# Stages 6 and 7 in one block: one pass for two norms, projections issued ahead of the last group's norm, and output and final norm per batch in rows of tokens

## The reference

```python
x = _layernorm(x + _L3_attn_ref(x, ...))     # stage 6
x = _layernorm(x + _L3_ffn_ref(x, ...))      # stage 7

# stage 6, _L3_attn_ref: 6 layers
for i in range(6):
    xn = ln(x, ln1_w[i], ln1_b[i])
    x = linear_attn(xn @ wq[i], xn @ wk[i], xn @ wv[i]) @ wo[i] + bo[i] + x
    xn = ln(x, ln2_w[i], ln2_b[i])
    x = leaky_relu(xn @ w1[i]) @ w2[i] + x

# stage 7, _L3_ffn_ref: q, k, v from the norm of x; tokens in quarters of 64 per batch,
# quarter e uses the first 128 / 2**e channels of its input
xn = ln(xe, norm_w, norm_b)                   # a norm of a value that was normed just before
q, k, v = (xn[..., :m] @ w[:, :m].T + b for w, b in ...)
attn_out = softmax(q @ k.T * 128 ** -0.5) @ v # 8 heads of 16
out = attn_out[:, sl, :m] @ o_w[:m, :m].T + o_b[:m]      # padded to 128
return out + x
```

## Time and profile before

| | us |
|---|---|
| time, median of 3 runs (lowest to highest) | 2009.62 (2007.04 to 2012.48) |
| the profiled execution: its time / its span in the trace | 2013.46 / 2011.7 |
| PE, DVE, ACT, POOL busy in the span | 1736.3, 1581.1, 1251.7, 360.0 |
| mean granted clock of TensorE | 0.87 |

### The profile page before, as it was taken

How to read it: one execution, slowest core, us unless ns; L and a number is a source line. 1 busy time by engine, 2 the same in 40 slices (tenths; PEclk the granted TensorE clock), 3 DMA queues, 4 the chain that set the end, 5 groups by cost and what they waited for, 6 DMA issues and landing times. The chain is left out here.

```text
span 2011.7 us, 46155 instructions
## 1 busy us (share of the span) xinstructions
PE 1736.3 (86%) x16491; PEld 1088.0 (54%) x16498; DVE 1581.1 (79%) x3789; ACT 1251.7 (62%) x3209; POOL 360.0 (18%) x476
## 2 busy tenths in 40 slices
PE   5999978866859999948769999999969999998685
PEld 4999953444534444426544444444436666665453
DVE  4444458988878999987879999999967887777663
ACT  5666637743425655556438888888856666665565
POOL 1000001200011111110001122212214343445111
PEclk7555568978869999979879999999979999999797
DMA  3200006300004444300026666666610000000000
GB/s 79 63 4 4 4 12 252 115 13 1 0 15 178 159 163 161 132 1 1 0 79 246 234 225 222 233 231 222 227 66 22 22 3 21 22 1 1 2 2 22
DMA packets 51669, 174.04 MB, mean 87 GB/s; under 512 B 7104, under 2 KB 32448, under 8 KB 34112
## 3 DMA queue, kind: packets, MB, share of 16 engines
q1 hardware_dynamic: 50368, 170.09, 23.4%
q10 hardware_dynamic: 1152, 1.90, 0.3%
HBM read 167.45 MB, written 2.95 MB: 85 GB/s over the span
## 5 line engine op out<-in xcount | busy, mean ns | idle before, releaser
L865 DVE TENSOR_TENSOR ps<-ps,m_comb 128x512 f32<-128x512 f32 x520 | 363.4, 699 | 23.9 <-DMA m_comb<-m_shares 7.2
L850 DVE TENSOR_TENSOR m_hwlo<-ps,m_hwhi 128x512 f16<-128x512 f32 x520 | 354.0, 681 | 0.3
L826 ACT ACTIVATE m_hwhi<-ps 128x512 f16<-128x512 f32 x520 | 308.2, 593 | 20.9 <-DVE ps L865 19.4
L832 ACT ACTIVATE ps<-ps 128x512 f32<-128x512 f32 x388 | 225.9, 582 | 81.7 <-PE ps L782 81.5
L782 PE MATMUL ps<-x_hi,m_whi 128*128 128x512 f16 x652 | 250.2, 384 | 8.5 <-DVE m_hwlo L850 4.6
L782 PE MATMUL ps<-x_lo,m_whi 128*128 128x512 f16 x652 | 250.1, 384 | 0.0
L782 PE MATMUL ps<-x_hi,m_wlo 128*128 128x512 f16 x652 | 249.8, 383 | 0.0
L755 POOL CAST m_whi<-m_stage 128x256 f16<-128x256 f32 (+1 forms) x130 | 55.2, 424 | 903.4 <-PE ps L788 633.0
L464 DVE TENSOR_TENSOR rn_s_lo<-rn_s_full,rn_s_hi 128x32 f16<-128x32 f32 x512 | 98.7, 193 | 133.0 <-ACT rn_s_full L421 133.0
L788 PE MATMUL ps<-m_hwhi,m_whi 128*128 128x512 f16 x520 | 197.7, 380 | 0.4 <-DVE m_hwlo L850 0.2
L788 PE MATMUL ps<-m_hwlo,m_whi 128*128 128x512 f16 x520 | 197.6, 380 | 0.0
(11 more groups left out here) (449 smaller groups left out, 4006.0 us busy)
## 6 DMA issues: line engine op xcount, KB each, us to landing
m_comb<-m_shares SPq DMA_DIRECT2D x128, 1024.0 KB, 5.1
m_stage<-in_m_w SPq DMA_DIRECT2D x97, 128.0 KB, 4.5
m_stage<-in_m_w SPq DMA_DIRECT2D x33, 192.0 KB, 4.6
kept_lj_w<-in_lj_w SPq DMA_DIRECT2D x6, 1024.0 KB, 5.0
kept_lq_w<-in_lq_w SPq DMA_DIRECT2D x1, 1600.0 KB, 7.8
kept_la_w<-in_la_w SPq DMA_DIRECT2D x1, 1280.0 KB, 5.4
rn_rows<-in_L_attn_rows SPq DMA_DIRECT2D x4, 256.0 KB, 4.3
rn_xs<-rn_xn_hi SPq DMA_DIRECT2D x32, 32.0 KB, 1.9
```

What stands on the lines that cost most here:

```text
L826: nc.scalar.activation(hw_hi[:, k % HB, :], weighted(k), ACT.Copy).then_inc(hi_done, 1)
L832: nc.scalar.activation(acted(k), ps[:, 4, :] if gated else bank(k), func).then_inc(act_done, 1)
L850: nc.vector.tensor_tensor(hw_lo[:, k % HB, :], weighted(k), hw_hi[:, k % HB, :], ALU.subtract)\
L865: nc.vector.tensor_tensor(weighted(k), bank(k), comb[:, s, n * QW:(n + 1) * QW], ALU.mult)\
```

## The change

Stages 6 and 7 become one block (`l3`); the barriers between them and the two calls of `layernorm_phase` at and behind stage 7 are gone. `l3_ffn` no longer opens a block but returns, per engine, two functions `fill` (one projection) and `step`, which `l3` calls.

- **Two norms in one pass.** Behind layer 6 each group gets two scales from one set of statistics: `rstd` for stage 7's normed input (the norm of a norm, in closed form) and `rstd2`, twice the plain one, for the residual. ACT normalises twice, into `rows2` (`x0` reused), which PE transposes back, and into `rows`, which stays in rows of tokens as the residual.
- **Projections ahead.** `LEAD` calls the first six projections and step 0 between turns of the pipeline. PE's projections wait for the halves of their group and for their banks.
- **Output in rows.** The output product has the attention's halves stationary (64 tokens) and 128 columns of weights moving. Per batch follow the residual, statistics and the last norm; POOL normalises batches 0 to 6, DVE batch 7, and SP stores 128 KB per batch. For batch 7 DVE also does `o` and its lower half.
- POOL clears `v` at the start of stage 6; the bias is added to the residual per batch. Buffers of stage 6 serve stage 7 (`spare`).

```diff
+        ffn = l3_ffn(nc, S, A, out, ctx, spare, spare_q, spare_c, rows, in_lo[0], in_y[0], res_on, nth)
+        LEAD = {(LAST, DEPTH - 1, 35): (0, 1), (LAST, DEPTH, 1): (2, 3), (LAST, DEPTH, 5): (4, 5)}
+        def lead(fill, step, event):
+            for n in LEAD.get(event, ()):
+                fill(0, *ffn.first[n])
+            if event == (LAST, DEPTH, 3):
+                step(0)
...
         def _(act):
...
                     act.wait_ge(in_aggr[s], nth(m, g))
+                    if layer == DEPTH:
+                        nc.scalar.activation(logv[:, tiles], mv[:, tiles, 1], ACT.Ln, bias=S.eps_ap(LN_EPS ** 2),
+                                             scale=1.0 + LN_EPS).then_inc(in_log[s], 1)
+                        nc.scalar.activation(logv2[:, tiles], mv[:, tiles, 1], ACT.Ln, bias=S.eps_ap(LN_EPS)).then_inc(log2_s, 1)
...
+                    if layer == DEPTH:
+                        act.wait_ge(log2_s, nth(0, g))
+                        nc.scalar.activation(rstd2[:, tiles], logv2[:, tiles], ACT.Exp, bias=S.eps_ap(LN2), scale=-0.5)\
+                            .then_inc(rstd2_s, 1)
...
+                    if layer == DEPTH:
+                        act.wait_ge(shift2_s, nth(0, g))
+                        for i in range(4 * g, 4 * g + 4):
+                            last = nc.scalar.activation(rows[:, cut(i, C)], top[:, i % 4 * C:(i % 4 + 1) * C], ACT.Identity,
+                                                        bias=shift2[:, i:i + 1], scale=rstd2[:, i:i + 1])
+                        last.then_inc(res_on, 1)
...
-                        last = nc.scalar.activation(xT[:, cut(g)], low, ACT.Copy)
+                        last = nc.scalar.activation(y[:, cut(g)], low, ACT.Identity, bias=ffn.shift, scale=ffn.gain)
...
+            for event in turns():
+                turn(*event)
+                lead(fill, step_on, event)
+            for s in range(1, ffn.steps):
+                step_on(s)
...
-        layernorm_phase(nc, S, S.xT, S.rT, gain=cols[:, 0:1], shift=cols[:, 1:2], pool=clear)
...
+        def fill(m, kind, n, bank):
+            pe.wait_ge(x_on, nth(DEPTH, m))
+            if m == 0 and bank in HOME:
+                pe.wait_ge(y_on_in, nth(DEPTH, HOME[bank]))
...
-                            last = products(nc, ps[:, 7, T + n * QT:T + (n + 1) * QT], weight(at), (o_hi[:, cut], o_lo[:, cut]),
-                                            first=(a == 0), last=(n > 0 or a == HG - 1))
+                        half, tile = slice(n % 2 * QT, (n % 2 + 1) * QT), slice(T + n // 2 * P, T + (n // 2 + 1) * P)
+                        last = products(nc, ps[half, 7, tile], (o_hi[:, cut], o_lo[:, cut]), weight(at),
+                                        first=(a == 0), last=(n > 0 or a == HG - 1))
...
+    def gpsimd(pool):
+            if (b := batch(s, 2)) is not None:
+                pool.wait_ge(res_on, nth(0, b // 2))
+                nc.gpsimd.tensor_tensor(rows[:, cut], rows[:, cut], y_b[:], ALU.add).then_inc(x2_s, 1)
...
+            if (b := batch(s, 11)) is not None and b < B - 1:
+                pool.wait_ge(fin_rstd, b + 1)
+                for i in range(TB):
+                    last = nc.gpsimd.tensor_scalar(tile, tile, mv[:, b % 2, i, 0:1], rstd[:, b % 2, i:i + 1],
+                                                   ALU.subtract, ALU.mult)
...
+    def vector(dve):
+            if (b := batch(s, 8)) == B - 1:
+                nc.vector.tensor_tensor(o[:], u_sb[:, b % 2].rearrange("p a t -> p (a t)"), rec[:], ALU.mult).then_inc(o_s, 1)
...
+            if (b := batch(s, 10)) is not None:
+                nc.vector.tensor_tensor(rows[:, cut], ps[:, 7, T:2 * T], rows[:, cut], ALU.add).then_inc(y_on, 1)
+                for i in range(TB):
+                    last = nc.vector.bn_stats(stats[:, b % 2, i, :], rows[:, b * T + i * P:b * T + (i + 1) * P])
+                for i in range(TB):
+                    last = nc.vector.bn_aggr(mv[:, b % 2, i, :], stats[:, b % 2, i, :])
...
+            sp.dma_start(tiles[b], rows[:, b * T:(b + 1) * T].rearrange("p (i c) -> p i c", c=C)).then_inc(stored, 16)
```

More of the change, by code:

```diff
@@ new lines, in store @@
+    def store(sp):
+        tiles = out.rearrange("b (i p) c -> b p i c", p=P)
+        for b in range(B):
+            if b < B - 1:
+                sp.wait_ge(fin_pool, b + 1)
+            else:
+                sp.wait_ge(fin_dve, 1)
+            sp.dma_start(tiles[b], rows[:, b * T:(b + 1) * T].rearrange("p (i c) -> p i c", c=C)).then_inc(stored, 16)
+        sp.wait_ge(stored, 16 * B)
+    stage = State()
+    stage.tensor, stage.scalar, stage.vector, stage.gpsimd, stage.store, stage.clear = tensor, scalar, vector, gpsimd, store, clear
@@ L2233, in build @@
+    stage.gain, stage.shift, stage.first, stage.steps = cols[:, 0:1], cols[:, 1:2], FIRST, STEPS
+    return stage
 def build(nc, A, out):
```

634 lines of the change are left out of this document (350 added, 284 removed).

## The result

The changed kernel takes 1986.59 us (median of 4 runs, 1984.46 to 1989.00); the kernel before took 2011.05 us beside it. The ratio is 0.9883, 95% interval 0.9864 to 0.9903: 24 us faster. Forecast were 1991 us and a range of 1984 to 2000, so time and sign lie inside; the forecast's own bounds for the sum, 1985 to 1995, hold it narrowly, and several of the terms miss. The profiled execution of the changed kernel took 1986.01 us with a span of 1984.2, that of before 2013.46 with 2011.7.

A forecast was written before the change was run, and what follows sets the result against it. The prediction took PE as nearly full in the steady attention, so the gain must come from the two seams: -13.2 + 2.0 - 7.7 = -18.9 us, from the median 2009.62 to 1990.7, given as 1991 us; range 1984 to 2000.

The forecast's parts named there:

- First seam: From stage 6's last residual to the maxima of pairs 0 and 1: done 13.2 us earlier, bounds -16 to -10.
- ACT ahead of the residual: First seam: extra normalising sets and small ACT work ahead of group 2's last piece make its residual 3.1 us later.
- my bound for a PE that keeps its clock, -16: First seam: if PE keeps full clock, 1.8 us of transposes and v products and 1.0 of first steps go.
- its last 1.0 us: First seam: 1.0 us added because the loop's first projection and scores may still run at the lower clock.
- Middle: Attention loop, batches 0 to 5: wider output product on PE costs +2.0 us in all, bounds 0 to +2.4.
- cost at nothing: Middle: DVE's statistics (0.7 us), ACT's small functions (0.5) and POOL's additions per batch fit into slack, so add no time.
- Tail: Behind the last exponential, a serial chain: 7.7 us less, bounds -8.7 to -6.9.
- the outputs of batches 6 and 7: Tail: both output products lie on the serial chain at the lower clock, +0.8 us each.
- The loaded loop: Rival: DVE's, ACT's and PE's additions all lie on a step's path, 8.4 + 2.8 us instead of 2.0; 2000 us; chance 0.11.
- Ahead is not early: Rival, first seam: q and k evictions hold back group 2's norm, about 5 us return; 1996 us; chance 0.10.
- POOL locks DVE: Rival, attention: POOL's 9.5 us of new time blocks DVE, which becomes the bound; 2000 us; chance 0.04.
- The slower clock: Rival, whole loop: PE stays below full clock after the wait ahead of group 2's norm; about 2065 us; chance 0.04.

The follow-up runs named there:

- res_once: Changed kernel without ACT's second set of normalising instructions; POOL makes the residual rows as twice the double norm's rows: 1981.41 us.
- the second execution: The changed kernel run and profiled once more, unedited, as reference for the edits beside it: median 1987.36 us.
- stats_twice: Changed kernel with DVE's two statistics and two aggregations and ACT's logarithm of the final norm issued twice in all eight batches: ratio to before 0.9875 to 0.9913.
- one_norm: Kernel before with stage 7's own norm folded into stage 6's last norm, projections still behind the barrier, old tail: 2003.74 us against 2007.90.
- b7_pool: Changed kernel with batch 7's product with the reciprocals, lower half and normalisations on POOL instead of DVE: ratio to before 0.9886 to 0.9918.
- tail_order: Changed kernel with the last quad's product u in bank 6, ahead of batch 6's output, and batch 6's logarithm and exponential later on ACT: 1984.46 us.
- all_three: Changed kernel with residual rows from POOL, last quad's product ahead of batch 6's output, and added matmuls in seam and tail: ratio to before 0.9855 to 0.9894.

## Why the prediction was right, and where not

The mechanism was right: the gain lies in the two seams and the middle got dearer. The time lies near the lower end of the forecast's own bounds; the terms did not cancel but mostly missed the same way, towards too small a gain. One reading of the earlier trace rows is wrong: in the 14.3 us of stage 7's own norm ACT is busy 7.43 us, as long as PE, and DVE 11.56; they are not idle there. No term used it.

*First seam, -13.2 us.* Measured -14.7 (41.11 to 26.40) and -16.6. Both parts of the working hold: ACT ahead of the residual +2.8 for +3.1 (res_once takes 2.6 of it back), and my bound for a PE that keeps its clock, -16, is the second execution. In the first profile the clock did fall, and the working without its last 1.0 us ends 26.9 us behind the mark (82.2 - 55.26); 26.40 were measured. So 0.5 of the 1.5 us missed is size, and the 1.0 for slow first steps came behind the maxima, not ahead of them: hence 14.8 us from residual to maxima, and 12.9 in the second profile, instead of 16 to 19. For the second profile the middle value failed on the step "I take the middle, because the trace shows PE at the lower clock each time that it has waited some us": in the second execution it had not fallen after 2.9 us of waiting. The 1.0 us for the first steps was too small where it did fall: 2.0 more were given back up to pair 7 (15.07 against 13.09 from maxima to maximum), 0.65 where it did not.

*Middle, +2.0 us.* Pairs 7 to 31 lost 1.4, and eight steps take 23.3 us on average for 22.8 (the sign said 22.2 to 23; the 22.2 was one stretch, not the average). The size holds by luck, the reason does not. I had charged the output product and nothing for the statistics. The step "per batch the output product has 15 matmuls of 128 instead of 64 columns" failed: the rows name 64 stationary columns, in pairs (x2), and the set of batch 6 lasts from 1969.33 to 1970.02 (1969.78 + 0.24), 0.69 us at full clock. Issued one behind the other 0.057 us apart, 15 products would take 1.0. A set of before takes 0.61 at full clock (1976.47 to 1977.08). At the lower clock it is 1.17 us (the last set, 1978.23 to 1979.40) for 0.98. So the additions are 0.1 and 0.2 us, not 0.4 and 0.8. Two products into different halves of the bank's partitions run at once. The Trainium skill ("TensorEngine Tiling (Array Packing)", "When to Use Tiling") says that 64 stationary columns allow two products side by side; the row agrees. The other step that failed is the statistics "cost at nothing" because "a pair's maximum is needed only two steps later". Each set on DVE delays the maximum queued behind it by 0.6 to 0.9 us; the step after it makes up all but 0.1 to 0.3 of this, and at pair 31, where the stretch ends, 0.6 is still open. Up to the last exponential the middle lost only 0.9. All other steps are those of before to 0.04 us. stats_twice, in which a second set costs 1.74 and 1.23 us by the same two measures, agrees. No run took the first set away, and that one_norm lost 1.2 us there without any statistics warns that such a small difference can have another source.

*Tail, -7.7 us.* Measured -10.4 (-10.0 in the second profile): -1.5 from the last exponential to the last residual, where the terms gave +0.6, and -9.0 behind it for -8.3. The term of the outputs of batches 6 and 7 ("at the lower clock: +0.8 each") is the one that was wrong, for the same reason: batch 6's set took 0.69 us at full clock for 0.98 at the lower one, batch 7's 1.17 for 0.98, together -0.1 instead of +1.6. `o` and its half on DVE, -1.0, hold (b7_pool: 1.4 with its handovers). The last store takes 2.2 us from DVE's end (1981.96) to 1984.2, not 2.9; it lies near the lower bound of 1.9. No run has the new tail alone; but one_norm, which keeps the old one, needs 26.1 us from the last exponential to the end, as before (26.4), and the changed kernel 15.9 and 16.4, so this gain does not come from the seam.

*Sum.* -18.9 forecast, -22.2 and -25.1 in the two profiles behind the mark, -24.5 between the medians beside each other. In the first profile the 3.3 us beyond the forecast are -1.5 in the seam, +0.9 in the middle and -2.7 in the tail; in the second the 6.1 us are -3.4, -0.4 and -2.3.

*Rivals.* The loaded loop is half true: additions cost up to 0.29 us per batch, not 1.4. Ahead is not early: the forecast 5 us did not come back, but what the lead itself gives, 1.2 to 3.6 us, stays open. POOL locks DVE: maxima take 1.22 us with and without POOL beside them; the casts' 0.15 us is all. The slower clock did appear in the kernels with the change, near the seam in most profiles for 3 to 14 us at a time and in the tail of all, but in none through the loop, where it was 1.00 from 46 to 106 us behind the mark.

## What to carry to other kernels

Before crediting a change, find the last event that it cannot touch and count from there: here the part ahead moves by 6 us, more than any single edit of the changed kernel. Near its ends, where engines take turns, price both levels of the clock rather than one, and compare two profiles of the same kernel before reading a few microseconds as an effect. Where an edit gives double what its rows allow, look for a partner that ran at the same clock: more than half of tail_order's 3.1 us was the clock. Work moved ahead pays where it fills a wait, but not on a queue that must itself wait for the engine being relieved.

## What was not expected of the hardware

- The granted clock of the same instructions differed between executions of one kernel: 0.55 and 0.50 against 1.00 over 14 us, worth 3.25 us. Ten added matmuls of 512 columns in a wait did not prevent a fall to 0.50 some 7 us later (all_three). What decides it stays open.
- Two sums over 128 partitions into halves of one bank, each of 64 columns, run side by side: 15 products in 0.69 us at full clock, against 0.61 before for as many with half the results.
- POOL takes 1.57 us for two 128x128 subtract-and-multiply instructions with column operands, but 0.73 for one 128x256 addition: twice as much for the same elements, of which the second instruction's own share is not known.
